# Diffusion and deformable convolution on one core: the first image's own sums in two halves, its force added by flips, one table for Ln and Exp, shorter position arithmetic, new orders

## The reference, cut to what is computed

```python
# layer 1, on the normalised image h (s0)
g, g1 = relu(bn(dwconv3x3(h, wg))), relu(bn(dwconv3x3(h, wg1)))
gy, gx = sobel(h)                                  # reflect padding
Dx, Dy = 1/(gy*gy/4 + 1), 1/(gx*gx/4 + 1)
E = 0.5*(roll(g,1,W) - roll(g,-1,W) + roll(g1,1,C) - roll(g1,-1,C)) * DT
D = 1/(1 + 2*Bx + 2*By)                            # Bx = Dx*DT, By = Dy*DT
for _ in range(5):
    prev = h
    h = D*(c0*h0 - 2*E*h + cm_x*roll(h,1,W) + cp_x*roll(h,-1,W) + cm_y*roll(h,1,C) + cp_y*roll(h,-1,C))
    h = h + D*(2*DT)*s0
    h0 = prev
x = x + relu(bn(h))
# layer 2, on the normalised x: 27 offset channels per pixel (9 y, 9 x, 9 masks)
# out[p] = sum over 9 taps of filt[k] @ (bilinear sample of x at p + tap + offset) * sigmoid(mask)
```

## Time and profile before

| | |
|---|---|
| runs | 807.9, 807.94, 808.3 us |
| the profiled execution | 803.14 us, its span 801.3 us |
| GpSimd (POOL) | busy 544.0 us; 568 gathers from 80.7 us on |
| TensorE (PE) | busy 669.2 us |
| VectorE (DVE) | busy 539.4 us |
| ScalarE (ACT) | busy 242.2 us |
| mean granted clock of TensorE | 0.904 |

### The profile page before, as it was taken

The page is one execution under the profiler, slowest core; times in us unless marked ns, Lnnn a source line. Parts: engine busy times, 40 slices in busy tenths (PEclk is TensorE's granted clock), DMA queues, the critical chain, the costliest instruction groups (busy, mean ns, idle before and its releaser), DMA issues.

```text
span 801.3 us, 15341 instructions
## 1 busy us (share of the span) xinstructions
PE 669.2 (84%) x4616; PEld 589.9 (74%) x4616; DVE 539.4 (67%) x906; ACT 242.2 (30%) x469; POOL 544.0 (68%) x583
## 2 busy tenths in 40 slices
...
GB/s 167 56 3 55 97 110 109 159 108 115 109 166 109 128 110 112 163 122 109 109 167 114 121 110 167 107 126 108 113 162 114 109 108 167 111 109 108 114 111 72
DMA packets 55146, 92.80 MB, mean 116 GB/s; under 512 B 13384, under 2 KB 35480, under 8 KB 55064
## 3 DMA queue, kind: packets, MB, share of 16 engines
...
q10 hardware_dynamic: 192, 0.15, 0.1%
...
## 4 chain that ended last, share of the span: by engine, by line
POOL 57%; issue 20%; PE 12%; DVE 7%; ACT 2%; DMA 1%; POOLq 0%; SPq 0%; DVEq 0%; ACTq 0%
POOL pixels L558 57%; PE banks L1150 9%; PE banks L1153 4%; DVE weighted L903 1%; DMA pixels<-table,index 1%; DVE banks L759 1%; DVE prod L778 0%; DVE prod L798 0%; DVE row_squares L582 0%; ACT coef_T L1051 0%; DVE prod L816 0%; DVE prod L779 0%; ACT sampled_T L1063 0%; DVE banks L760 0%; DMA taps<-taps_in 0%
## 5 line engine op out<-in xcount | busy, mean ns | idle before, releaser
L558 POOL DMA_INDIRECT pixels<-table,index x568 | 538.7, 948 | 247.6 <-issue 172.4
L1153 PE MATMUL banks<-const,weighted 128*128 128x128 f32 x1280 | 194.5, 308 | 62.8 <-DVE weighted L903 49.5
L903 DVE TENSOR_TENSOR weighted<-pixels,banks 128x2304 f32<-128x2304 f32 (+1 forms) x65 | 161.2, 2480 | 115.7 <-DMA pixels<-table,index 111.8
L1153 PEld LDWEIGHTS banks<-const,weighted 128*128 128x128 f32 x1280 | 169.6, 163 | 73.9 <-DVE weighted L903 53.8
L1063 ACT ACTIVATE sampled_T<-banks 128x512 f32<-128x512 f32 (+1 forms) x128 | 55.7, 435 | 335.1 <-PE banks L1153 334.3
L1153 PE MATMUL banks<-const,prod 128*128 128x128 f32 x816 | 109.9, 278 | 19.3 <-DVE prod L778 12.9
L1153 PEld LDWEIGHTS banks<-const,prod 128*128 128x128 f32 x816 | 90.7, 143 | 28.2 <-DVE banks L760 14.1
L1150 PE MATMUL banks<-conv_w,xT 128*128 128x64 f32 (+2 forms) x576 | 97.7, 325 | 0.7 <-ACT banks L1040 0.7
L1150 PEld LDWEIGHTS banks<-conv_w,xT 128*128 128x128 f32 x576 | 91.4, 191 | 7.0 <-ACT banks L1040 1.6
L1150 PE MATMUL banks<-filt,sampled_T 128*128 128x64 f32 x640 | 87.0, 286 | 7.2 <-ACT sampled_T L1063 7.2
L1150 PEld LDWEIGHTS banks<-filt,sampled_T 128*128 128x128 f32 x640 | 81.5, 202 | 13.5 <-ACT sampled_T L1063 11.5
...
## 6 DMA issues: line engine op xcount, KB each, us to landing
...
pixels<-table,index POOLq DMA_INDIRECT x568, 2.7
...
```

Of the source, the lines that this page charges most:

```text
L558: pool.indirect_dma_start(out=pixels[:, col % NB, k, :], out_offset=None, in_=table[0:(u + 1) * TY * TX, :], in_offset=bass.IndirectOffset ...
L903: return dve.tensor_tensor(weighted[:, col % 2, :, a:b, :].rearrange("p q k c -> p k q c"), entries.rearrange("p k (q c) -> p k q c", c=C) ...
L1153: return pe.matmul(dst, data, moved, start=start, stop=stop, is_transpose=True, skip_group_check=True)
```

## The change

Orders: all three lists are new. For the first image they read, before (-) and after (+):

```diff
 DVE
-rows1+0 mean1+0 bnpa+0 rowsq1+0 bnpb+0 var1+0 bnpc+0 shw+0 scale1+0 dif+0 cells+0 edges1+0 bnout+0 den+0 diff+0
-force+0 dgx+0 coefx+0 dgy+0 px0+0 coefy+0 py0+0 vown+0 prod0+0 coef0+0 seed1+0 px1+0 py1+0 prod1+0 seed2+0 px2+0
...
-py2+0 prod2+0 seed3+0 px3+0 py3+0 prod3+0 seed4+0 px4+0 py4+0 prod4+0 rows1+1 mean1+1 final+0 rows2+0 mean2+0
-rowsq1+1 var1+1 rowsq2+0 var2+0 scale2+0 scale1+1 edges2+0 edges1+1 samp1+0 samp2+0 rowc+0 den+1
+rows1+0 mean1+0 rows1+1 rowsq1+0 var1+0 bnpa+0 bnpb+0 bnpc+0 scale1+0 shw+0 dif+0 cells+0 edges1+0 bnout+0 den+0
+diff+0 force+0 dgx+0 coefx+0 dgy+0 coefy+0 px0+0 py0+0 vown+0 prod0+0 seed1+0 coef0+0 px1+0 py1+0 prod1+0
+seed2+0 px2+0 py2+0 prod2+0 seed3+0 px3+0 py3+0 prod3+0 seed4+0 px4+0 py4+0 prod4+0 mean1+1 rows1+2 final+0
+rows2+0 mean2+0 rowsq1+1 rowsq2+0 var1+1 var2+0 scale2+0 edges2+0 scale1+1 samp1+0 edges1+1 rowc+0 samp2+0 den+1
 ACT
-squares1+0 root1+0 biasc+0 cb1+0 main1+0 gxs+0 cb0+0 gys+0 log+0 exp+0 ... tF+0 tL+0 tR+0 tB+0 tC+0 tO+0 tU+0
+squares1+0 root1+0 init+0 biasc+0 cb1+0 main1+0 cb0+0 gys+0 gxs+0 log+0 exp+0 ... tF+0 tL+0 tR+0 tB+0 tU+0 tC+0 tO+0
 PE
-sum1+0 sq1+0 biasm+0 turn+0 gx+0 gy+0 conv0a+0 conv0b+0 conv1a+0 conv0+0 conv1b+0 conv1+0 init+0 edge+0 fF+0
-fL+0 stx0+0 own+0 sty0+0 fR+0 sto0+0 fB+0 fC+0 fO+0 fU+0 stx1+0 sty1+0 sto1+0  stx2+0 sty2+0 sto2+0 stx3+0
-sty3+0 sto3+0 stx4+0 sty4+0 sto4+0 sum1+1 back+0 sum2+0 sq1+1 sq2+0 halo+0 turn2+0 turn+1 off+0 gy+1 row+0
+sum1+0 sq1+0 biasm+0 turn+0 gy+0 gx+0 conv0a+0 conv0b+0 conv1a+0 conv0+0 conv1b+0 conv1+0 ownx+0 edge+0 fF+0
+fL+0 owny+0 stx0+0 sty0+0 fR+0 sto0+0 fB+0 fU+0 fC+0 stf1+0 fO+0 stx1+0 sty1+0 sto1+0 stf2+0 sum1+1 stx2+0
+sty2+0 sto2+0 stf3+0 stx3+0 sty3+0 sto3+0 stf4+0 stx4+0 sty4+0 sto4+0 back+0 sum2+0 sq1+1 sq2+0 turn2+0 off+0
+turn+1 row+0
```

The code:

```diff
-WARM_UP = (6, 4, 6)
+WARM_UP = (6, 1, 6)
...
 def seed(u, m):                                    # DVE
+                if u == 0:
+                    dve.tensor_tensor(target(m), (c0[:, :], c0_T)[1 - m % 2], target(m), ALU.mult).then_inc(s_seeded, 1)
+                    return
...
+            def first_force(m):                    # PE, pieces stf1 to stf4
+                pe.wait_ge(s_seeded, m)
+                if m % 2:
+                    pe.wait_ge(*emptied(0, "tF"))
+                src = force_T if m % 2 else force[:, :]
+                for j in range(PAIRS):
+                    add(pair(target(m), PAIRS - 1 - j), pair(src, j), eye)
...
 def positions(u):
-                seq(dve.tensor_copy(pos_int[:, :], ps))
-                seq(dve.tensor_copy(lo, pos_int[:, :]))
-                seq(dve.tensor_tensor(ab, lo, ps, ALU.is_gt))
-                seq(dve.tensor_tensor(lo, lo, ab, ALU.subtract))
+                seq(dve.tensor_scalar(lo, ps, -0.5, ROUND, ALU.add, ALU.add))
+                seq(dve.tensor_scalar(lo, lo, -ROUND, None, ALU.add))
...
 ACT
-            functions = {"root1": ACT.Sqrt, "log": ACT.Ln, "exp": ACT.Exp, "root2": ACT.Sqrt, "sig": ACT.Sigmoid}
+            sets = {"root1": "sqrt_and_others", "root2": "sqrt_and_others", "log": "natural_log_exp_and_others",
+                    "exp": "natural_log_exp_and_others", "sig": "sigmoid_and_others"}
-                    act.activation(unused[:, i:i + 1], one, after)
+                    act.preload_act_table_set(after)
+                elif name == "init":               # image 0: h set by ACT, no longer by a matmul
+                    act.wait_ge(s_xn, 1)
+                    act.wait_ge(s_preset_bank, 1)
+                    act.activation(source(0), xn[:, :], ACT.Copy).then_inc(s_init, 1)
...
 turn (PE), for edges2: the halo goes to the same bank, DVE copies it in edges2; pieces halo and haloc are gone
-                flip(bank(u, edges)[:, P:2 * P], src[:, 0:P], M["next"]).then_inc(s_full, 1)
+                ins = flip(bank(u, edges)[:, P:2 * P], src[:, 0:P], M["next"])
+                if edges == "edges2":
+                    ins = mm(bank(u, edges)[:, 2 * P:2 * P + C], M["halo"], src[:, 0:C], True, True)
+                ins.then_inc(s_full, 1)
...
 turned_edges (DVE), before the last of its three copies
+                    if what == "edges2" and dh == ROW_ORDER[-1]:
+                        dve.tensor_copy(xn2[:, WS + 1, :], bank(u, what)[:, 2 * P:2 * P + C])
...
 write_table (SP)
-                sp.wait_ge(*emptied(u, "halo"))
+                sp.wait_ge(*emptied(u, "edges2"))
...
 own_sums is split: own_sums_x (4 matmuls of gate 0), own_sums_y (4 of gate 1)
-                pe.wait_ge(s_gated, 2 * u + 2)
-                pe.wait_ge(s_force, u + 1)
+                if u:
+                    pe.wait_ge(s_gated, 2 * u + 2)
+                    pe.wait_ge(s_force, u + 1)
+                else:
+                    pe.wait_ge(*emptied(u, "edges1"))
...
 PE, after sum1 of image 0: a second bank is written once, for ACT's init
-                        mm(bank(0, "conv1"), ones[:, :], x1[0][:, :], True, True).then_inc(s_preset_bank, 1)
+                        for of_engine in (bank(0, "conv1"), source(0)):
+                            ins = mm(of_engine, ones[:, :], x1[0][:, :], True, True)
+                        ins.then_inc(s_preset_bank, 1)
```

More of the change, by code:

```diff
@@ L82 @@
[L82 to L106, removed]
-ACT_PIECES = """
@@ L108 @@
[L108 to L117, removed]
@@ L135 @@
-fL+0 stx0+0 own+0 sty0+0 fR+0 sto0+0 fB+0 fC+0 fO+0 fU+0 stx1+0 sty1+0 sto1+0  stx2+0 sty2+0 sto2+0 stx3+0
-sty3+0 sto3+0 stx4+0 sty4+0 sto4+0 sum1+1 back+0 sum2+0 sq1+1 sq2+0 halo+0 turn2+0 turn+1 off+0 gy+1 row+0 conv0a+1 gx+1
-conv0b+1 conv0+1 init+1 conv1a+1 conv1b+1 conv1+1 edge+1 own+1 fR+1 stx0+1 sty0+1 fL+1 fU+1 sto0+1 fB+1 stx1+1
-fO+1 sty1+1 fF+1 sto1+1 fC+1 sum1+2 stx2+1 flip0@0 sty2+1 sto2+1 flip1@0 stx3+1 sty3+1 filt@0 sto3+1 flip0@1
-stx4+1 sty4+1 sto4+1 flip1@1 back+1 filt@1 flip0@2 sum2+1 flip1@2 filt@2 sq2+1 flip0@3 sq1+2 halo+1 flip1@3
@@ new lines @@
+edges1+2 rows1+3 rowc+1 samp2+1 mult@5 add@0 mult@6 den+2 diff+2 force+2 dgx+2 coefx+2 dgy+2 coefy+2 mult@7
+vown+2 px0+2 py0+2 coef0+2 prod0+2 seed1+2 mult@8 px1+2 py1+2 prod1+2 seed2+2 px2+2 py2+2 prod2+2 seed3+2 add@1
+px3+2 py3+2 prod3+2 seed4+2 mult@9 px4+2 py4+2 prod4+2 mult@10 mean1+3 final+2 rows2+2 mean2+2 rowsq1+3 rowsq2+2
+var1+3 var2+2 scale2+2 edges2+2 scale1+3 mult@11 samp1+2 edges1+3 rowc+2 samp2+2 mult@12 add@2 mult@13 mult@14
+den+3 diff+3 force+3 dgx+3 coefx+3 dgy+3 coefy+3 mult@15 vown+3 px0+3 py0+3 coef0+3 prod0+3 seed1+3 mult@16
@@ new lines @@
+px1+3 py1+3 prod1+3 rows1+4 seed2+3 px2+3 py2+3 prod2+3 seed3+3 add@3 px3+3 py3+3 prod3+3 seed4+3 mult@17 px4+3
+py4+3 prod4+3 mult@18 mean1+4 final+3 rows2+3 mean2+3 rowsq1+4 rowsq2+3 var1+4 var2+3 scale2+3 edges2+3 scale1+4
+mult@19 samp1+3 edges1+4 rowc+3 samp2+3 mult@20 add@4 mult@21 mult@22 den+4 diff+4 force+4 dgx+4 coefx+4 dgy+4
+coefy+4 mult@23 vown+4 px0+4 py0+4 coef0+4 prod0+4 seed1+4 mult@24 px1+4 py1+4 prod1+4 rows1+5 seed2+4 px2+4
+py2+4 prod2+4 seed3+4 add@5 px3+4 py3+4 prod3+4 seed4+4 mult@25 px4+4 py4+4 prod4+4 mult@26 mean1+5 final+4
@@ new lines @@
+rows2+4 mean2+4 rowsq1+5 rowsq2+4 var1+5 var2+4 scale2+4 edges2+4 scale1+5 mult@27 samp1+4 edges1+5 rowc+4
+samp2+4 mult@28 add@6 mult@29 mult@30 den+5 diff+5 force+5 dgx+5 coefx+5 dgy+5 coefy+5 mult@31 vown+5 px0+5
+py0+5 coef0+5 prod0+5 seed1+5 mult@32 px1+5 py1+5 prod1+5 rows1+6 seed2+5 px2+5 py2+5 prod2+5 seed3+5 add@7
+px3+5 py3+5 prod3+5 seed4+5 mult@33 px4+5 py4+5 prod4+5 mult@34 mean1+6 final+5 rows2+5 mean2+5 rowsq1+6
+rowsq2+5 var1+6 var2+5 scale2+5 edges2+5 scale1+6 mult@35 samp1+5 edges1+6 rowc+5 samp2+5 mult@36 add@8 mult@37
```

234 lines of the change are left out of this document (129 added, 105 removed).

## The result

The changed kernel takes 809.64 us (median of 20 runs, 808.28 to 814.43), the kernel before beside it on the same chip 807.1 (20 runs, 804.05 to 808.43). The ratio is 1.0038, 95% interval [1.0025, 1.005]: **slower** by 3.1 us, between 2.0 and 4.0, as the ratio has it; the medians alone differ by 2.5. The profiled execution took 810.39 us with a span of 808.6. Against the profile of before (803.14, quicker than all of its 20 runs) that is 7.3 us, of which 4.2 lie ahead of the first gather and 2.8 behind the last; the runs, with 3.1, say that not all of this is the change.

A forecast was written before the change was run, and what follows sets the result against it. GpSimd's gapless 568 gathers bound the kernel: start of the first gather + 710.5 + 10.1 us. Ten items on the path to that gather sum to +1.8, 807.9 + 1.8 = 809.7 us; range 806.2 to 812.2.

The forecast's parts named there:

- item 9: Halo in `edges2`, `off` ahead of `turn+1`: index gains, table lands later and decides; -0.2 us, bounds -2.1 and +1.4.
- rival A: The forecast itself: the wait for image 1 costs what the steps give back, +1.0 to +2.6 us; chance 0.50.
- rival B: Idle PE throttled in full ahead of `turn`, losing 2.6 us instead of 0.9: +3.5, 811.4 us; chance 0.14.
- Item 1: DVE's start: `rows1+1` ahead of `rowsq1+0` makes DVE wait for image 1's load; +4.0 us.
- Item 2: `bnpa`, `bnpb`, `bnpc` between `var1` and `scale1` put nine small instructions between variance and reciprocal; +1.4 us.
- Items 3 and 4: `shw` behind `scale1` holds up PE's `biasm` and `turn`, +0.6 us; `gy` ahead of `gx` saves PE's idling, -0.3.
- Item 10: PE's clock around the idle time ahead of `turn`: partly lost at half clock; +0.9 us, between 0 and 2.6.
- Items 5 to 7: Image 0's layer 1: `init` on ACT, -1.1 us; own sums in halves, -0.7; force by flips replacing DVE adds, -2.1.
- Item 8: `rowsq2+0` straight behind `rowsq1+1`, so two trips over PE to the variance overlap; -0.7 us for xn2.
- Rival E: Image 1 is there when DVE asks at 7.5: wait costs 0.7, not 4.0; -1.5 us in all; chance 0.12.
- Rival F: PE's clock falls during the steps, now nearly all flips: +2 us for each of four, +8, 816; chance 0.03.
- rival D: Table lands no later than the index, its DMAs faster issued in one piece: -0.1 us, 807.8; chance 0.07.

The follow-up runs named there:

- e3: Kernel before with one piece moved: `rows1+1` behind `mean1+0`, ahead of `rowsq1+0`, as in the change; 813.1 us, ratio 1.007.
- e10: Changed kernel with unread matmuls ahead of `sum2+0`, `sq1+1`, `sq2+0`, `turn2+0` and, filling PE's gap, `off+0`; 807.18 us, ratio 1.0006.
- e2: e1 with `bnpa`, `bnpb`, `bnpc` and `shw` also back in their old places; 805.13 us, ratio 0.9975 to the kernel before.
- e1: Changed kernel with one piece moved: `rows1+1` behind `bnout+0`, no longer ahead of `rowsq1+0`; 803.94 us, ratio 0.9973 to the kernel before.
- e5: Changed kernel with 5, 4 and 8 units of unread matmuls ahead of `sum2+0`, `sq1+1` and `turn2+0`; 804.78 us, ratio 0.998 to the kernel before.
- e9: Changed kernel with `turn+1` again ahead of `off` and `scale1+1` ahead of `edges2`, the halo staying in `edges2`; 808.88 us, ratio 1.0027.
- e7: e2 with the force of image 0 added by DVE again in steps 1 to 4, no flips for it; 805.72 us, ratio 1.0003.
- e6: Kernel before with unread matmuls among the flips of the last two columns; 804.39 us, ratio 0.9981.
- e11: Kernel before with the unread matmuls of e10 and nothing of the change; 808.66 us, ratio 1.0028.
- e4: e2 with 5, 4 and 8 units of unread matmuls ahead of `sum2+0`, `sq1+1` and `turn2+0`; 797.89 us, ratio 0.9887 to the kernel before.
- e8: e2 with the unread matmuls of e10 (2 units, not 5, ahead of `off+0`) and those of e6; 796.66 us, ratio 0.9885.

## Why the prediction was right in sum and wrong in item 9

809.7 was forecast and 809.64 measured, which is luck: the kernel before, 807.94 in its first three runs, has 807.1 in twenty. By the ratio it is +3.1 us where +1.8 was forecast: inside the range, slower as forecast (0.44, against 0.43 for no change), but outside rival A's +1.0 to +2.6 and nearer to B's +3.5. And the steps did not add up as written. From landmark to landmark, between the two profiles:

| stretch | forecast | measured |
|---|---|---|
| to xn (items 1, 2) | +5.4 | 16.57 - 11.93 = +4.6 |
| xn to first convolution (3, 4, 10) | +1.2 | 8.4 - 6.1 = +2.3 |
| convolution to relu (5, 6, 7) | -3.9 | 37.2 - 41.3 = -4.1 |
| relu to xn2 (8) | -0.7 | 8.5 - 9.2 = -0.7 |
| xn2 to first gather (9) | -0.2 | 14.3 - 12.2 = +2.1 |
| sum | +1.8 | +4.2 |

- **Item 1** was the right mechanism. The wait was 4.59 us, and cost 3.25 on the path instead of 4.0, because DVE could go on at 10.9 here and not at 11.8. In e3 it was 11.6 and in e10 11.9: the landing of a load that nobody waited for before can only be read to about a microsecond. Rival E (image 1 there at 7.5) is refuted.
- **Item 2** gave 1.91 - 0.53 = 1.4, as forecast; what e2 won back, 1.0 with item 3, is within what two profiles differ by.
- **Item 10** was mis-sized. 0.9 was taken between 0 and 2.6. The stretch at 0.50 lasted from 11.5 to 21.7 and cost 2.4: xn to the first convolution took 8.4, and 6.0 in e1, which has items 3 and 4 and no such stretch. Items 3 and 4, forecast at +0.3, then came to -0.1. This is nearly rival B, with 2.6. But it varies: 8.4 in e5 and 8.1 in e9, 7.1 in e3, and 6.0 in e10, where the clock came back at 16.5. I had read the warm-ups as cover for the gap; but the gap of 4.63 us lies ahead of them, and it is item 1's own wait. The two should have been one item: undone together in e1, they were 5 us, about their forecast sum (4.9).
- **Items 5 to 7** are confirmed as a sum by the trace, item 7 by itself in e7 (about 1.9 against 2.1). Rival F is refuted: the clock was 1.00 from 24 to 66 with the force's flips inside, and in the steps of all eight profiles with these flips. It fell in the steps of kernels without them: in e7, and in e6 and e11 for 7 us from 52 on, though not in before and e3. The trace points the other way from F, and flips that keep PE busy may be worth more than their 2 us; no run isolates that. The Trainium skill (TensorE: Matmul & The Clock Gate, PE-mode transpose) warns that transposes don't count as a busy PE in the same way; in these steps, nearly all flips, the trace doesn't bear that out.
- **Item 8** is confirmed to 0.1.
- **Item 9 is the step that failed**, in both of its halves. "The table decides": SP did write 3.0 behind xn2 (3.2 forecast), and the table's last packets ended 10.0 behind xn2 (10.7 forecast), but the index decided. "The index is at xn2 + 9.1": it came at xn2 + 13.4. Of the 2.1 that it was to gain, the shorter positions gave theirs (1.7 from offsets to index, 2.4 before). The six flips out of the way gave nothing: the offsets began 4.0 behind xn2, and 3.9 in the kernel before, for `off` now waits 1.19 us for the last copy of `edges2`. And the forecast took the offsets at the speed of the kernel before, 4.9; they ran at 1.2 GHz throughout and took 7.7.
- What I missed is that `turn+1`, which item 9 booked as six flips out of the way, kept PE at work in front of `off`. With the flips back (e9) the clock, low since 65.6, returned at 75.8; without them it stayed low to 90.0. Item 10 looked at the clock only ahead of `turn`. The earlier trace rows held the hint: 0.50 in 69 to 74 with the twelve flips in it (69.06 to 71.83), 1.00 from 76.5 on. Why the clock returns in one case and not in the other stays open: the gap of 1.19 us alone does not say it (e4).
- Where the clock was up for the offsets the index came at xn2 + 9.3 in e4 and + 8.6 in e8 and e10, as item 9 has it (9.1), and the gather at xn2 + 9.5 to 10.2 rather than 11.9. SP's write began 2.2 behind xn2 in e8 and e10, as the flips ran at full speed, and GpSimd started 7.3 after it, where 7.5 + 0.3 + 0.9 = 8.7 was forecast. That the table lands no later than it is needed, rival D's condition, is so in the changed kernel, by over 3 us, and nearly so in these three; D's time did not come because the index was late. The Trainium skill (DMA: Bandwidth & Descriptors, Anatomy of one DMA — SWDGE (gpsimd) path) puts most of about 2 us of a DMA issued by GpSimd down to the write receipt. SP issues these, and in e8 the gather that needs the table began 0.7 behind its last packet, so no delay near 2 us is in it.
- The costs put at nothing held, but barely. Image 1's index was ready at 170.1 and its gathers began at 174.1: 4.0 us to spare out of 12.2 (4.5 in e1, 9.0 in e9). Another loss of that size would stall there.

So the profiles do not bear the sum out: 2.4 us more were lost ahead of the first gather than forecast, and the 10.1 us behind the last gather, which the prediction took as given, were 12.9. That the runs show only 3.1 of the profiles' 7.3 goes with the profile of before, which was quicker than all of its 20 runs; which part of the 7.3 is chance is not shown.
